# A transformer block on one core: the first attention gathers two head groups per PSUM bank

## What is computed

```python
qm = _split_heads(q @ Wq.T + bq)
km = _split_heads(k @ Wk.T + bk)
vm = _split_heads(v @ Wv.T + bv)
scores = jnp.einsum('bnlh,bnph->bnlp', qm, km) / np.sqrt(HEAD_DIM)
scores = jnp.where(mask, scores, MASK_FILL)
attn = jax.nn.softmax(scores, axis=-1)
out = jnp.einsum('bnlp,bnph->bnlh', attn, vm)
...
x = x + out @ Wo.T + bo
```

## Time and profile before

| | before |
|---|---|
| median of 3 runs | 594.29 us (592.61 to 595.97) |
| profiled execution, its own time | 594.72 us |
| span of that execution | 592.9 us |
| PE busy | 566.6 us (96%) |
| DVE busy | 399.4 us (67%) |
| ACT busy | 323.7 us (55%) |
| POOL busy | 104.6 us (18%) |
| mean granted TensorE clock | 0.994 |

### The profile page before, as it was taken

One profiled execution on the slowest core, in us unless ns is written; L12 is line 12 of the kernel. 1 busy time (PEld: TensorE's weight loads), 2 busy tenths in 40 slices (PEclk: granted clock), 3 DMA queues, 4 the chain that ended last, 5 costly groups with the idle time before them and its releaser, 6 DMA issues.

```text
span 592.9 us, 8098 instructions
## 1 busy us (share of the span) xinstructions
PE 566.6 (96%) x2512; PEld 372.9 (63%) x2512; DVE 399.4 (67%) x1265; ACT 323.7 (55%) x566; POOL 104.6 (18%) x120
## 2 busy tenths in 40 slices
PE   2799999999999999999999999999899999999997
PEld 2666667665666666656676567565667766676664
DVE  4889899783212444648557675778889899677564
ACT  1478687867445466844775458854385342343221
POOL 3102020000211210242122315235200011100000
PEclk9899999999999999999999999999899999999999
DMA  2601000030211120111101021053211332342441
GB/s 78 233 19 28 1 10 2 2 143 19 58 49 36 38 71 19 35 38 36 36 35 36 2 64 36 20 175 112 89 72 53 112 109 87 113 141 67 134 138 40
DMA packets 23306, 38.35 MB, mean 65 GB/s; under 512 B 3776, under 2 KB 9536, under 8 KB 22880
## 3 DMA queue, kind: packets, MB, share of 16 engines
q1 hardware_dynamic: 22832, 37.44, 19.9%
q10 hardware_dynamic: 432, 0.40, 0.3%
HBM read 36.45 MB, written 1.38 MB: 64 GB/s over the span
## 4 chain that ended last, share of the span: by engine, by line
PE 84%; DVE 7%; ACT 4%; issue 3%; DMA 1%; POOL 1%; ACTq 0%; DVEq 0%
PE ps L1682 17%; PE ps L1493 10%; PE ps L1495 9%; PE ps L1494 9%; PE ps L1852 9%; PE ps L1569 4%; PE ps L1488 4%; PE ps L1589 3%; PE ps L1500 2%; PE ps L1604 2%; PE ps L1601 2%; PE ps L1759 2%; PE ps L1739 1%; PE ps L1749 1%; DVE NM L1156 1%
## 5 line engine op out<-in xcount | busy, mean ns | idle before, releaser
L1493 PE MATMUL ps<-xThi,w1s 128*128 128x512 f32 x256 | 144.4, 564 | 2.1 <-DVE h L1445 2.1
L911 ACT ACTIVATE h<-ps,early 128x512 f32<-128x512 f32 x128 | 86.8, 687 | 79.5 <-PE ps L1495 65.7
L1682 PE MATMUL ps<-h,w2s 128*128 128x512 f32 x256 | 122.1, 594 | 0.2 <-DVE ty L1245 0.2
L1495 PE MATMUL ps<-xTlo,w1s 128*128 128x512 f32 x256 | 101.4, 396 | 0.0
L1494 PE MATMUL ps<-xThi,w1s 128*128 128x512 f32 x256 | 100.8, 394 | 0.0
L1002 ACT ACTIVATE s<-ps 128x512 f32<-128x512 f32 x68 | 40.7, 599 | 101.2 <-PE ps L1495 100.9
L1493 PEld LDWEIGHTS ps<-xThi,w1s 128*128 128x128 f32 x256 | 48.6, 190 | 36.5 <-issue 16.9
L1682 PEld LDWEIGHTS ps<-h,w2s 128*128 128x128 f32 x256 | 46.7, 189 | 33.4 <-issue 24.1
L1445 DVE TENSOR_TENSOR h<-s,ps 128x512 f32<-128x512 f32 x68 | 46.5, 684 | 28.7 <-PE ps L1495 25.8
L1494 PEld LDWEIGHTS ps<-xThi,w1s 128*128 128x128 f32 x256 | 48.8, 190 | 25.9 <-issue 21.4
L1852 PE MATMUL ps<-h,w2s 128*128 128x512 f32 x128 | 64.2, 594 | 0.9 <-DVE h L1451 0.9
(11 more groups left out here) (264 smaller groups left out, 884.8 us busy)
## 6 DMA issues: line engine op xcount, KB each, us to landing
CB<-ct_rows SPq DMA_DIRECT2D x128, 128.0 KB, 2.9
WB<-wt_rows SPq DMA_DIRECT2D x32, 256.0 KB, 3.2
w2s<-w_dram SPq DMA_DIRECT2D x2, 2048.0 KB, 8.1
raw<-gu_dram SPq DMA_DIRECT2D x4, 512.0 KB, 5.5
x_in<-x_dram SPq DMA_DIRECT2D x4, 256.0 KB, 2.8
w2s<-dn_dram SPq DMA_DIRECT2D x1, 1024.0 KB, 7.2
out_dram<-ty SPq DMA_DIRECT2D x4, 256.0 KB, 2.9
late<-late_dram SPq DMA_DIRECT2D x1, 608.5 KB, 7.5
```

Source lines behind the costliest of these rows:

```text
L911: nc.scalar.activation(h32[:, c % HR, :], bank[c % 2], ACT.Gelu, bias=b1T[:, c:c + 1]).then_inc(b_gelu.sem, 1)
L1493: M(dst, w[0], xThi[:, x, :], start=start, stop=False)
L1495: return M(dst, w[0], xTlo[:, x, :], start=False, stop=stop)
L1682: M(bank[2], w2s[:, c * P:(c + 1) * P], h32[:, c % HR, :], start=(c % 4 == 0), stop=(c % 4 == 3)).then_inc(b_y.sem, 1)
```

## The change

Two groups, g = 2h and 2h+1, now share bank 4. The even group's values and ones sit in columns 0 to 15 of a head's 32, the odd group's in 16 to 31, with zeros in the other half. The even group's products overwrite the bank, the odd group's add to it. Then one ACT copy to OZ, one set of four transposes and one reciprocal (of 32 denominators per row instead of 16) serve both groups; the two multiplications stay, one per group. So of each batch's four copies, 16 transposes and four reciprocals, two, eight and two are left. In exchange, VM is filled by four POOL copies per batch instead of one (and is zeroed whole at the start), VT by eight DVE copies instead of four, and the ones are set by two memsets and eight copies instead of one and four.

The tables of all five engines are new numbers as well, so the order of steps changes in every stage. One line of PLAN_POOL and one of PLAN_DVE stand below for all of them.

```diff
...
-    "constants": [[0, 15, 32, 60, 289, 340, 368]],
+    "constants": [[0, 15, 32, 60, 838, 889, 939]],
-    "constants": [[450, 1105, 1181, 1194, 1202, 1243, 1251, 1259, 16819, 19591]],
+    "constants": [[0, 1037, 1047, 1066, 1080, 1203, 1329, 1344, 13819, 15282]],
...
-    rz = sb_a("rz", [P, NT, HG])
+    rz = sb_a("rz", [P, NT, HG, 2])
...
-    a_mk, a_km, a_kn, a_vtail = sig("a_mk", 2), sig("a_km", 1), sig("a_kn", 4), sig("a_vtail", HG)
-    a_vmain, a_vtm = sig("a_vmain", 1), sig("a_vtm", 1)
+    a_mk, a_km, a_kn, a_vtail = sig("a_mk", 2), sig("a_km", 1), sig("a_kn", 4), sig("a_vtail", 2 * HG)
+    a_vmain, a_vtm = sig("a_vmain", NG), sig("a_vtm", 1)
...
-    a_pv, a_oz, a_ozt_ps, a_on = sig("a_pv", NG), sig("a_oz", NG), sig("a_ozt_ps", NG), sig("a_on", 2 * NG)
+    a_pv, a_oz, a_ozt_ps, a_on = sig("a_pv", NG), sig("a_oz", NG // 2), sig("a_ozt_ps", NG // 2), sig("a_on", 6)
...
-    NZERO, NONE, NPAD, NLATE = 7, 2 + 1 + HG + 1, 3, 2
+    NZERO, NONE, NPAD, NLATE = 7, 2 + 2 + 2 * HG + 1, 3, 2
...
-            nc.gpsimd.memset(VM[:, :, :, 2 * HD:VB], 0.0).then_inc(zeros.sem, 1)
+            nc.gpsimd.memset(VM[:], 0.0).then_inc(zeros.sem, 1)
...
             pool.wait_ge(a_v32.sem, a_v32.at(b, 1))
             vh = v32[:, 0, :].rearrange("p (g j d) -> p g j d", j=HG, d=HD)
-            nc.gpsimd.tensor_copy(VM[:, :, :, 0:HD], vh).then_inc(a_vmain.sem, 1)
+            for g in range(NG):
+                o = VB // 2 * (g % 2)
+                nc.gpsimd.tensor_copy(VM[:, g, :, o:o + HD], vh[:, g]).then_inc(a_vmain.sem, 1)
...
-            yield
-            act.wait_ge(a_pv.sem, a_pv.at(b, g + 1))
-            copy(OZ[:], bank[4]).then_inc(a_oz.sem, 1)
+            if g % 2:
+                yield
+                act.wait_ge(a_pv.sem, a_pv.at(b, g + 1))
+                copy(OZ[:], bank[4]).then_inc(a_oz.sem, 1)
...
             dve.wait_ge(zeros.sem, NZERO)
-            V.memset(VM[:, :, :, HD:2 * HD], 1.0).then_inc(ones.sem, 1)
+            for k in range(2):
+                o = VB // 2 * k + HD
+                V.memset(VM[:, k:NG:2, :, o:o + HD], 1.0).then_inc(ones.sem, 1)
             for j in range(HG):
                 yield
-                q, c = slice(TP * j, TP * j + TP), VB * j + HD
-                V.tensor_copy(VT[q, :, c:c + HD], valid[q, 1:2].unsqueeze(2).to_broadcast([TP, NG, HD])).then_inc(ones.sem, 1)
+                for k in range(2):
+                    q, c = slice(TP * j, TP * j + TP), VB * j + VB // 2 * k + HD
+                    V.tensor_copy(VT[q, k:NG:2, c:c + HD], valid[q, 1:2].unsqueeze(2).to_broadcast([TP, NG // 2, HD])).then_inc(ones.sem, 1)
...
                     yield
-                q, o = slice(TP * j, TP * j + TP), VB * j
-                V.tensor_copy(VT[q, :, o:o + HD], vt[q, :, j, :]).then_inc(a_vtail.sem, 1)
+                for k in range(2):
+                    q, o = slice(TP * j, TP * j + TP), VB * j + VB // 2 * k
+                    V.tensor_copy(VT[q, k:NG:2, o:o + HD], vt[q, k:NG:2, j, :]).then_inc(a_vtail.sem, 1)
...
-        def normalise(b, g):
-            src = four(bank[4])
-            yield
-            dve.wait_ge(a_ozt_ps.sem, a_ozt_ps.at(b, g + 1))
-
-            V.reciprocal(rz[:], src[:, :, HD::VB]).then_inc(a_on.sem, 1)
-            yield
-            dve.wait_ge(a_on.sem, a_on.at(b, 2 * g + 1))
-            if b:
-                dve.wait_ge(a_ot_ps.sem, a_ot_ps.at(b, 0))
-            V.tensor_tensor(ON[:, :, g, :].rearrange("p i (h d) -> p i h d", d=HD),
-                            src.rearrange("p i (h d) -> p i h d", d=VB)[:, :, :, 0:HD],
-                            rz[:].unsqueeze(3).to_broadcast([P, NT, HG, HD]), ALU.mult).then_inc(a_on.sem, 1)
+        def normalise(b, h):
+            src = bank[4].rearrange("p (i j k d) -> p i j k d", i=NT, j=HG, d=VB // 2)
+            yield
+            dve.wait_ge(a_ozt_ps.sem, a_ozt_ps.at(b, h + 1))
+            V.reciprocal(rz[:], src[:, :, :, :, HD]).then_inc(a_on.sem, 1)
+            for k in range(2):
+                yield
+                if k == 0:
+                    dve.wait_ge(a_on.sem, a_on.at(b, 3 * h + 1))
+                    if b:
+                        dve.wait_ge(a_ot_ps.sem, a_ot_ps.at(b, 0))
+                V.tensor_tensor(ON[:, :, 2 * h + k, :].rearrange("p i (h d) -> p i h d", d=HD), src[:, :, :, k, 0:HD],
+                                rz[:, :, :, k:k + 1].to_broadcast([P, NT, HG, HD]), ALU.mult).then_inc(a_on.sem, 1)
...
             if g == 0:
-                pe.wait_ge(a_vmain.sem, a_vmain.at(b, 1))
-                pe.wait_ge(a_vtail.sem, a_vtail.at(b, HG))
+                pe.wait_ge(a_vmain.sem, a_vmain.at(b, NG))
+                pe.wait_ge(a_vtail.sem, a_vtail.at(b, 2 * HG))
             turn = (b * NG + g) * NU
-            claim(4)
+
+            if g % 2 == 0:
+                claim(4)
             pe.wait_ge(a_exp.sem, turn + HG)
             for j in range(HG):
-                M(bank[4][VB * j:VB * j + VB, :], VM[:, g, j, :], P32[(turn + j) % PR], start=True, stop=False)
+                M(bank[4][VB * j:VB * j + VB, :], VM[:, g, j, :], P32[(turn + j) % PR], start=(g % 2 == 0), stop=False)
             yield
             pe.wait_ge(a_exp.sem, turn + NU)
-            M(bank[4], VT[:, g, :], P32[(turn + HG) % PR], start=False, stop=True).then_inc(a_pv.sem, 1)
-            read_by(4, a_oz, a_oz.at(b, g + 1))
-            yield
-            claim(4)
-            transpose4(bank[4], OZ[:].rearrange("p (i t) -> p i t", i=NT)).then_inc(a_ozt_ps.sem, 1)
-            read_by(4, a_on, a_on.at(b, 2 * (g + 1)))
+            M(bank[4], VT[:, g, :], P32[(turn + HG) % PR], start=False, stop=(g % 2 == 1)).then_inc(a_pv.sem, 1)
+            if g % 2:
+                read_by(4, a_oz, a_oz.at(b, g // 2 + 1))
+                yield
+                claim(4)
+                transpose4(bank[4], OZ[:].rearrange("p (i t) -> p i t", i=NT)).then_inc(a_ozt_ps.sem, 1)
+                read_by(4, a_on, a_on.at(b, 3 * (g // 2 + 1)))
...
-            pe.wait_ge(a_on.sem, a_on.at(b, 2 * NG))
+            pe.wait_ge(a_on.sem, a_on.at(b, 6))
...
```

More of the change, by code:

```diff
@@ L132 @@
[L132 to L136 removed]
+    "constants": [[0, 15, 32, 60, 838, 889, 939]],
+    "norm_a": [[710, 737], [1760, 1787], [4380, 4407], [7330, 7357]],
@@ new lines @@
+    "masks": [[894, 1030], [2709, 2744], [4960, 5201], [7857, 7875]],
+    "keys": [[1094, 1139, 1172, 1218, 1296], [1889, 2830, 2863, 3118, 3165], [5246, 5377, 5410, 5822, 5935], [7972,
+        8506, 8659, 8869, 8916]],
+    "values": [[1263, 1748, 1786, 2695, 2716, 2730], [4663, 4819, 4932, 4946, 5322, 5480], [7474, 7777, 7814, 7828,
+        7843, 7894], [10481, 10604, 10788, 10989, 11003, 11017]],
+    "queries": [[1412, 1484, 1546, 1560], [3493, 3565, 3628, 3949], [6047, 6246, 6670, 6683], [8733, 9207, 9270, 9283]
+        ],
@@ new lines @@
+    "biased": [[720], [2961], [3434], [6107]],
+    "split0": [[3020, 3641, 7035, 7095, 7590, 9958, 10544, 11928]],
+    "maxima": [[1812, 1850, 1922, 1960, 2015, 2053, 2107, 2146, 2196, 2216], [2224, 2269, 2358, 2397, 2486, 2525, 2579,
[9 rows of a table added]
+    "normalise": [[3701, 3726, 3930], [5087, 5112, 5132], [6819, 6877, 6896], [7908, 7933, 7953], [9651, 9676, 9708],
+        [10721, 10746, 10765], [12305, 12330, 12350], [13411, 13436, 13456]],
+    "output": [[5538], [8348], [11140], [13747]],
+    "norm_b": [[5857, 7274, 9165, 9644, 9696, 10056, 10075, 10427], [11319, 11435, 11684, 12047, 12066, 13475, 13494,
+        13832], [16146, 17133, 19242, 19710, 19729, 19807, 19826, 20219], [21269, 21874, 23467, 24872, 26208, 26938,
+        27048, 27100]],
@@ new lines @@
+    "queries": [[1631, 1926, 2183, 3578], [4129, 4961, 5327, 6174], [6841, 7754, 8046, 8941], [9467, 10614, 10787,
+        11732]],
+    "keys": [[1401, 1484], [3752, 3873], [6053, 6590], [9010, 9654]],
+    "maxima": [[1770, 1792, 1863, 1901, 1972, 2011, 2065, 2103], [2158, 2227, 2288, 2319, 2425, 2447, 2537, 2582],
[7 rows of a table added]
+    "scores": [[2244, 2371, 2402, 2485, 2559, 2599], [2715, 2919, 2942, 3076, 3202, 3228], [3532, 3668, 3691, 3796,
[5 rows of a table added]
+    "values": [[2764, 2965], [3309, 3433, 3622], [3974, 4173], [4692, 4816, 5005], [5582, 5787], [6272, 6416, 6724],
+        [6942, 7113], [7503, 7655, 7844], [8418, 8790], [9108, 9313, 9585], [9756, 9960], [10344, 10468, 10657],
+        [11184, 11388], [11830, 12035, 12238], [12445, 12615], [13022, 13157, 13336]],
@@ new lines @@
+    "output": [[5206, 5429], [7999, 8144], [10834, 11030], [13487, 13637]],
+    "prepare_b": [[10932, 11565, 12763], [14400, 15053, 18788], [20445, 23193, 25452], [27513, 28055, 30625]],
+    "first": [[12915, 13253, 13727, 13796, 13950, 14019, 14260, 14329, 14444, 14915, 14984, 15143, 15211, 15586, 15655,
[8 rows of a table added]
+    "weights": [[13394], [19817], [26508], [33134]],
+    "second": [[13548, 13864, 14088, 14174, 14516, 14657, 14743, 14829, 15283, 15369, 15455, 15723, 15950, 16036,
[8 rows of a table added]
```

(2 more changed lines are left out.)

215 lines of the change are left out of this document (91 added, 124 removed), and 178 rows, old and new, of tables (PLAN_ACT, PLAN_DVE, PLAN_PE, PLAN_SP).

## The result

The kernel before: 594.63 us (15 runs, 592.61 to 595.97). The changed kernel: 597.07 us (15 runs, 595.64 to 598.36). The ratio is 1.0041, 95% interval 1.0028 to 1.0054: slower by 0.4%, inside the 0.5% that one measurement tells from no change, but on the other side of zero than the forecast of 587.2 us, and above its range. The profiled execution took 595.89, its span is 594.1 (before: 594.72 and 592.9).

The account below looks back on a forecast made before the run. PE was taken to set the time wherever it is fed, with DVE near only in stage A. Transposes -3.5, ACT -0.8 and start -2.8 sum to -7.1 us, from 594.29 to 587.2 us; range 582.7 to 591.4.

Parts of the forecast that it names:

- Order in stages B to D: Stages B to D: nothing added or removed; the 3.5 us lost where POOL's difference meets DVE at 421.7 us stay, 0.
- The slower rival: POOL's differences, second and third back to back, make gate or value products late, 3.5 us each; up to 597.7; chance 0.05.
- It decides from the second: Claim that the slower case counts from two stalls of 3.5 us, which give back the 7.1 us gain but for 0.1.
- The sign that I had named for being wrong: Behind 350 us: more than one PE wait above 1 us beside a POOL difference, or a second half-clock stretch there.
- Start, -2.8: Kernel start: layer norm statistics no longer wait for the mask's cast, biased queries at 13.8 instead of 16.56: -2.8 us.
- Transposes, -3.5: Stage A, PE: 32 of 64 OZ transposes go, eight sets at the chain's 0.44 us each: -3.5 us.
- The rival that DVE sets stage A's pace: Stage A: DVE, not PE, is the bound; missing transposes leave only holes, VT copies cost 0.7; 591.4 us; chance 0.14.
- The price by the mean duration, 8.8 us: Stage A: 32 transposes priced at about 275 ns each would be worth 8.8 us; the prediction did not use it.
- Copies of VT and VM, 0: Stage A: extra copies, 2.8 us on DVE (VT) and at most 3.5 on POOL (VM), costed at 0.
- at most the 258 again: Stage A, DVE: the eight remaining reciprocals, twice as wide, would take at most 258 ns again.
- the +0.7 to +2.8 that I gave its queue: Stage A: DVE's net extra work from fewer reciprocals and more VT copies, +0.7 to +2.8 us, costed at 0 beside PE.
- ACT, -0.8: Stage A: eight OZ copies leave ACT, so half of PE's 1.7 us of waits for ACT goes: -0.8 us.
- the sum of 7.1: Whole kernel: the predicted gain, transposes -3.5, ACT -0.8 and start -2.8, together -7.1 us.

Follow-up runs that it names:

- s7: The changed kernel with the five weight differences on DVE instead of POOL, at the same numbers in DVE's table: 590.77 us, ratio 0.9942.
- s4: The kernel before with only the start reordered: mask's cast behind the first layer norm's steps, POOL's three memsets behind its power: 591.82 us, ratio 0.9951.
- s6: The change's code with the tables of the kernel before, except the start, which has the new order: 592.01 us, ratio 0.9957.
- s12: s6 with VM and VT at a pitch of 144 columns per group, so one copy does what four (VM) or two (VT) did: 591.59 us, ratio 0.9938.
- s9: The changed kernel with each of its eight sets of four OZ transposes done twice, 32 more: 598.23 us, ratio 1.0057.
- s13: The changed kernel with POOL's second and third differences apart and later, and two of stage B's last sums behind norm2b: 590.45 us, ratio 0.9935.

## Why the prediction was wrong

**The step that failed is "Order in stages B to D ... I keep these 3.5 us: 0".** That sum held for the one stall I had priced, which came again: a wait of 2.0 us at 424 and 3.4 us of half clock. But the two differences that moved made a new stall of 8.0 us in front of norm. The slower rival had the mechanism and the instructions right, POOL's second and third difference back to back, and I gave it 0.05. It had the place and the size wrong: not gate products at 3.5 us each, but one chain of 128x4 steps in which every step pays for a whole POOL instruction. "It decides from the second" was wrong too: one such stall was enough. The sign that I had named for being wrong came true: two waits above 1 us behind 350 us, 5.4 and 2.0, each beside POOL's differences, and a second stretch of half clock. I argued against it from PE's waits of the kernel before, but those say nothing of this place, where POOL was empty and 0.47 us were to spare. DVE's own rows of the kernel before would have told it. Of the tile ln_n_t (minimum, median, maximum ns) it had

```profile
L406 DVE TENSOR_TENSOR ln_n_t<-ln_n_t,ln_n_ve x12: 155/163/2311, 247.0 to 497.9; 128x4 f32<-128x4 f32 x12
```

a step of 0.16 us that once took 2.31, beside POOL's difference at 409.3, where PE had other work. I had looked only at the wide product L1352. Nor is it so that nothing on POOL yields to DVE: beside DVE's difference in s7 POOL's two sums took 3.52 us instead of 2.66.

**Start, -2.8:** right. It is -3.1 by the time of s4, and -3.1 in the change at the first maxima product (17.19 us, before 20.28). In s6 that product comes 0.55 us later than in s4, but 0.42 of it is there before the added copies, at PE's transposes of xn (9.62 against 9.20). The chain of the changed kernel, first 20 us, against the earlier trace rows:

```profile
0.72 3.19 DMA x_in<-x_dram
...
3.94 0.88 DVE ln_a_st L393 x4
...
7.49 0.80 DVE ln_a_t L407
...
9.68 1.12 PE ps L1493 x4
```

Statistics at 3.94 (4.1 to 4.6 forecast), transposes at 9.68 (9.2 to 9.6); the first QS at 16.54 (before 17.2). One step was not foreseen: L407, 0.80 us, is held beside two of the moved memsets of POOL, which I had put out of the way. PE's longest wait, 6.4 us for the mask's DMA ahead of its first instruction (now 5.7), is missing where I list its waits; the sum does not use it.

**Transposes, -3.5:** too much, and it depends on the order. Their busy time went as forecast (now L1493 with OZ, against the earlier trace rows):

```profile
L1493 PE MATMUL ps<-early,OZ 128*128 128x128 f32 x32 | 4.9, 276 | 0.0
```

but they are worth 0.1 us in the old order and 2.3 in the new. The rival that DVE sets stage A's pace fits s6, where maxima and VT take 10.7% of the chain. In s12, without the doubled copies, the maxima hold 5.4% (s4: 4.1%) and ACT's QS 1.6%, and still nothing is gained. Whether that is DVE, bank 4 held for two groups or an order fitted to the old durations stays open. The price by the mean duration, 8.8 us, is refuted by s9: 32 more cost 2.3 at the end of stage A.

**Copies of VT and VM, 0:** wrong by about 1 us. Against the earlier trace rows:

```profile
L1176 DVE RECIPROCAL rz<-ps x8: 344/352/358, 37.2 to 136.7; 128x32 f32<-128x32 f32 x8
...
L1117 DVE COPY VT<-vtm x32: 153/164/187, 17.2 to 113.2; 32x16 f32<-32x16 f32 x32
...
L757 POOL COPY VM<-v x16: 204/209/462, 18.3 to 109.1; 128x32 f32<-128x32 f32 x16
```

A copy of half the width takes nearly as long (164 against 172 ns), and DVE's idle time elsewhere in the 120 us was no cover for it. A reciprocal twice as wide takes 352 ns, not "at most the 258 again": the eight cost 2.8 us against 4.1, so DVE saves 1.3 there and pays 2.5 for VT, a net of 1.2 inside the +0.7 to +2.8 that I gave its queue. The error was to let idle time cover it.

**ACT, -0.8:** nothing of it is seen. From 20 to 140 us PE's waits for ACT are 0.6 + 0.5 + 0.2 = 1.3 us (QS, h, ty in front of L1594) against 1.7, but those 1.7 hold the wait for the first QS, 0.7 us at 20.28, and the earlier start has only moved this wait out of the window:

```profile
17.19 0.56 PE L1574 MATMUL ps<-KS,QS 128*128 128x320 f32 x2 [0.81 <-ACT QS L798]
```

With it there are 2.1 us now.

**The order of stage A:** not in the sum at all, and by the difference between s6 and the change the new tables are worth 5.9 us there, up to 2.3 of them what the missing transposes are worth in them. At the end of stage A the sum of 7.1 is nearly met, 147.6 - 139.9 = 7.7, but by other terms than mine. Three small waits of the new order at 253, 343 and 378 us then take 2.2 back; I had none of them, and two are again DVE steps held by POOL. s13, the change without its collision, lands at 590.45, 3 us above the forecast, and its ratio of 0.9935 has the sign that was forecast.
